# A graph network kernel: one-hots of source and destination made and stored during the dense product, marks summed as rows

## The chip, the cores and the metric

The kernel runs on one core of a Trainium2 chip. The metric is the device time of one execution in microseconds (us). The core has five engines that run side by side: TensorE (PE; its weight loads are PEld), VectorE (DVE), ScalarE (ACT), GpSimd (POOL) and SyncE (SP), which only issues DMAs. An engine works through its own instructions in order; between engines only semaphores order anything.

## The reference

A network of four layers on one graph of 3125 nodes (256 features) and 50000 edges, sorted by destination. Cut to what matters here:

```python
x = _layernorm(x + _L0(x, src, dst, edge_weight, ...))
x = _layernorm(x + _L1(x, ..., edge_attr_3, edge_index))
x = _layernorm(x + _L2(x, edge_index, ...))
x = _layernorm(x + _L3(x, src, dst, ...))

def _L0(x, edge_row, edge_col, edge_weight, weight, bias):
    gathered = edge_weight[:, None] * x[edge_col]
    neigh = segment_sum(gathered, edge_row, num_segments=3125)
    return x @ weight[:256] + neigh @ weight[256:] + bias

def _L1(...):   # attention with 8 heads, the alpha of an edge:
    alpha = sum(h[src] * a_src) + sum(h[dst] * a_dst) + sum(relu(edge_attr @ edge_W.T + edge_b) * h[dst])
    alpha = where(alpha >= 0, alpha, 0.2 * alpha)
    ...         # softmax over the edges of a destination, then the weighted sum of h[src]
```

`_L2` is one plain graph convolution and two attention layers with 4 heads, `_L3` three layers of plain neighbour sums with dense layers between them.

## The kernel before, in words

Layer 0 is computed as a dense product: the 3125 x 3125 matrix of edge weights is built in HBM (`t_w`) and multiplied with x. A second matrix, of edge counts (`t_adj`), serves the plain sums of `_L2` and `_L3`. Both are filled by scatters: an edge that stands for its pair of nodes writes the sum over all edges of this pair. So the stages are, in this order:

**Marks (L1860 to L1895, L888 to L899, L1309 to L1313).** The 50000 edges lie in 98 quads of 4 x 128. For a quad, `compare` on VectorE (and, from quad FIRST = 28 on, on ScalarE for the fourth block) holds the keys of all 512 edges (`wide_key`, loaded by SP from `t_key`, two quads in 512 KB) against the key of each edge: `same_key`, 4 x [128 x 512] in bf16. TensorE multiplies it with `values` (a one and three bf16 parts of the weight): 16 matmuls [128 x 128] by [128 x 4]. `summed` on VectorE reduces them to `w_sum` and `counts` and signals `w_summed`, once a quad.

**Weight scatter (L703).** POOL zeroes nothing itself; `t_w` is zeroed by 13 DMAs of ScalarE. POOL issues 391 indirect DMAs of 128 sums each. Their order (`w_order`) goes by groups of 8 quads: first the first block of each of the 8 quads, then the second, and so on; each waits for `w_summed` of its quad. At most 8 are under way.

**Own product (L906) and pair product (L884).** x times the first half of the weights, then, for 26 tiles of 128 rows of `t_w` (1.6 MB each, loaded by SP at L518 into a ring of four buffers, from the fifth on after `w_out` of two pairs before), 13 pairs of tiles x 13 blocks = 169 blocks. A block is two fp32 matmuls, each two records in the trace; VectorE adds it into `neigh` (L2217). `fold(0)` (L1933, L1934) on VectorE stands between the two and signals `folded0`.

**Zeroing of t_adj (L1333) and adjacency (L720).** ScalarE issues 35 DMAs of 640 KB, ten at once after its last `compare`, the others each after some blocks of the pair product. When all 35 have landed (`adj_zero`) and the counts are there, POOL scatters the counts: 391 indirect DMAs. After them come its gathers.

**First look-up (`look_up`, `encoded`, `edge_scores`).** For every four steps (of 128 edges; 104 times four) SP loads the source and destination numbers, spread over all partitions (`t_hi`, `t_drel`, 128 KB each), ScalarE turns them into one-hots by Abs and Relu (L1362, L1365, and L1366 for an fp32 copy of the destination half), SP stores the bf16 ones as `t_hot` for the later look-ups, and TensorE multiplies node values with them. `t_lo` holds the upper parts of the source numbers, spread by 27 copies from HBM to HBM (L494), which SP issues ahead of its first load of `t_w`.

SP's order around the change: key loads, `t_drel`, `t_hi`, `t_lo1`, the 27 copies, the 26 tiles of `t_w`, then the look-up's loads.

## Time and profile before

| | |
|---|---|
| three runs, median (lowest to highest) | 5571.05 us (5562.35 to 5572.14) |
| the profiled execution's own time | 5553.82 us |
| its span, first to last instruction | 5552.0 us |
| mean granted TensorE clock | 0.792 of full speed |
| busy: PE, PEld, DVE, ACT, POOL | 57%, 35%, 41%, 27%, 37% |
| DMA | 531 MB, 96 GB/s over the span |

Busy is the share of the span in which the engine had an instruction under way. The end of a matmul is modelled in these records, so the time at which a matmul's result was really there is read from the instruction that waited for it. "idle before" and the releaser after an arrow say how long an engine stood still before an instruction and what ended that; "issue" means nothing that the profile shows, and "remote" a source that it doesn't know, which in loops can be another engine of the same core. SPq and ACTq are issues of DMAs.

### The profile page before, as it was taken

To read this page: it belongs to the slowest core of one execution; us is meant where nothing else is said; L and a number is where in the kernel's file an instruction comes from. 1 tells how busy PE (TensorE), PEld (TensorE's weight loads), DVE (VectorE), ACT (ScalarE), POOL (GpSimd) and SP (SyncE) were. 2 spreads that over 40 slices of the span, in tenths; PEclk is the share of its full clock that TensorE was granted. 3 is DMA by queue.
4 is the path that set the end of the run, shared out by engine and by line. 5 is a ranking of instruction groups with operands and counts; after the bars stand their busy time and mean duration, and the time that the engine had idled before them with its cause. 6 is when DMAs were issued, how large, how long until landed. Compare 5 with 4: busy or idle time off the path is not lost. (4 is left out here: it accounts for less than half of the span.)

```text
span 5552.0 us, 64271 instructions
## 1 busy us (share of the span) xinstructions
PE 3182.6 (57%) x16684; PEld 1923.3 (35%) x16685; DVE 2287.2 (41%) x5611; ACT 1485.8 (27%) x3107; POOL 2063.3 (37%) x2093
## 2 busy tenths in 40 slices
PE   2111495332569955457603645771465565999998
PEld 2111342110447733234602522340343333444444
DVE  6222241001359974456202744770475568020213
ACT  0122100000359943235100133550023346030212
POOL 4666406777120056652273056207315540000000
PEclk9999897555779976677756866885676776999999
DMA  9211461000345532232513400014633331313131
GB/s 382 99 40 40 158 253 65 24 21 0 103 124 149 149 88 85 84 90 78 189 33 84 124 21 22 10 37 122 191 103 97 105 118 61 105 61 105 60 109 38
DMA packets 321424, 531.29 MB, mean 96 GB/s; under 512 B 140575, under 2 KB 204664, under 8 KB 317556
## 3 DMA queue, kind: packets, MB, share of 16 engines
q1 hardware_dynamic: 206233, 309.28, 18.0%
q0 software_dynamic: 80624, 130.79, 8.5%
q10 hardware_dynamic: 34381, 89.16, 4.2%
q8 instruction: 66, 1.08, 0.1%
q14 instruction: 120, 0.98, 0.1%
HBM read 410.68 MB, written 121.87 MB: 96 GB/s over the span
## 5 line engine op out<-in xcount | busy, mean ns | idle before, releaser
L1377 ACT ACTIVATE onehot<-iota,drel 128x128 f32<-128x128 f32 x1248 | 381.7, 388 | 1674.4 <-PE ps L1025 762.5
L1102 PE MATMUL ps<-shared_sb,onehot 128*128 128x264 f32 (+1 forms) x1600 | 594.3, 489 | 351.6 <-issue 202.2
L2147 DVE TENSOR_TENSOR accum<-accum,ps 128x264 f32 (+1 forms) x1248 | 527.8, 423 | 493.7 <-issue 315.3
L1162 PE MATMUL ps<-score_sb,shared_sb 128*128 128x512 f16 (+1 forms) x3150 | 628.2, 360 | 20.5 <-DVE shared_sb L2179 20.1
L749 POOL DMA_INDIRECT score_sb<-table,src_x x192 | 200.3, 1043 | 904.0 <-issue 456.5
L1102 PEld LDWEIGHTS ps<-shared_sb,onehot 128*128 128x128 f32 x1600 | 314.0, 228 | 632.4 <-issue 563.5
L720 POOL DMA_INDIRECT t_adj<-counts,early_sb x391 | 400.6, 1025 | 322.8 <-DMA t_adj<-onehot 203.3
L703 POOL DMA_INDIRECT t_w<-early_sb x391 | 390.5, 999 | 232.1 <-DVE counts L1872 131.4
L749 POOL DMA_INDIRECT shared_sb<-table,src_x x360 | 340.3, 945 | 229.2 <-PE ps L1102 119.3
L1162 PEld LDWEIGHTS ps<-score_sb,shared_sb 128*128 128x128 bf16 x3150 | 298.0, 99 | 342.9 <-DVE shared_sb L2179 14.6
L730 POOL TENSOR_SCALAR onehot<-iota,carry_d 98x512 bf16<-98x512 f32 x28 | 43.6, 1561 | 967.3 <-PE ps L1179 804.2
L2217 DVE TENSOR_TENSOR accum<-accum,ps 128x512 f32<-128x512 f32 (+1 forms) x156 | 103.9, 667 | 600.9 <-remote 425.6
L793 POOL DMA_INDIRECT resid_sb<-table,src_x x224 | 212.5, 949 | 361.2 <-DVE shared_sb L2133 243.7
L1002 PE MATMUL ps<-not_lo,lo_hot 128*128 128x400 bf16 x416 | 136.4, 369 | 345.6 <-DVE score_sb L1977 179.0
L1977 DVE TENSOR_REDUCE score_sb<-ps 128x400 f32 x208 | 119.5, 574 | 383.7 <-remote 310.8
L2133 DVE TENSOR_TENSOR shared_sb<-shared_sb,ps 128x256 f32<-128x256 f32 x512 | 211.5, 413 | 83.3 <-issue 55.3
L1023 PE MATMUL ps<-score_sb,onehot 128*128 x832 | 223.1, 412 | 36.5 <-issue 30.0
L897 PE MATMUL ps<-accum,shared_sb 128*128 x784 | 47.6, 171 | 337.7 <-DVE counts L1872 237.6
L749 POOL DMA_INDIRECT resid_sb<-table,src_x x168 | 158.9, 946 | 205.9 <-DMA t_resid<-resid_sb 114.9
L2402 DVE TENSOR_TENSOR accum<-accum,ps 128x1024 f32<-128x1024 f32 (+1 forms) x21 | 23.2, 1107 | 484.2 <-PE ps L1179 484.0
L884 PE MATMUL ps<-resid_sb,score_sb 128*128 128x512 f32 (+1 forms) x336 | 157.6, 614 | 107.5 <-issue 67.1
L1476 ACT ACT_TABLE_LOAD x1 | 1.3, 1283 | 803.5 <-DVE small L1912 803.5
(416 smaller groups left out, 5978.5 us busy)
## 6 DMA issues: line engine op xcount, KB each, us to landing
score_sb<-t_adj SPq DMA_DIRECT2D x105, 640.0 KB, 3.8
accum<-t_hot SPq DMA_DIRECT2D x208, 256.0 KB
t_w<-onehot ACTq DMA_DIRECT2D x13, 3200.0 KB
t_hot<-shared_sb SPq DMA_DIRECT2D x104, 256.0 KB
t_adj<-onehot ACTq DMA_DIRECT2D x35, 640.0 KB
shared_sb<-t_adj SPq DMA_DIRECT2D x35, 640.0 KB, 9.6
resid_sb<-t_w SPq DMA_DIRECT2D x12, 1600.0 KB
accum<-t_hi SPq DMA_DIRECT2D x104, 128.0 KB
```

What stands on the lines that cost most here:

```text
L703: pool.indirect_dma_start(t_w, bass.IndirectOffsetOnAxis(ap=w_x[:, j:j + 1], axis=0), w_sum[:, j:j + 1], None).then_inc((moved + gath)[n % ...
L720: pool.indirect_dma_start(t_adj, bass.IndirectOffsetOnAxis(ap=adj_x[:, j:j + 1], axis=0), counts[:, j:j + 1], None).then_inc((moved + gath ...
L749: pool.indirect_dma_start(to[:, u, 0:w], None, tab, bass.IndirectOffsetOnAxis(ap=src_x[:, step:step + 1], axis=0)).then_inc(landing[0], 16)
L793: pool.indirect_dma_start(x_rows[n % (RG[1] // HU)][:, u, :], None, table[1], bass.IndirectOffsetOnAxis(ap=src_x[:, n * HU + u:n * HU + u ...
L884: mm = pe.matmul(ps[:, m % 8, at:at + now.stop - now.start], lhs, w_ring[t % 4][0:EQ if t == NT else P, now], start=(t == 2 * i), stop=(t ...
L1002: pe.matmul(ps[:, b if k == 0 else q % 2, 0:n_to * NT * H], lo_hot[:, q, :], not_lo[:, to, :].unsqueeze(2).to_broadcast([P, n_to, H, NT]), ...
L1023: mm = pe.matmul(ps[:, 4 + j, 0:GW], hot, hrows[:, bass.ds(at[q * QU + j], 1), :], start=True, stop=True)
L1102: pe.matmul(ps[:, RING[(HU * h + u) % len(RING)], 0:w], onehot[:, h % 2 * HU + u, :], around[g][place(g, i, h)][:, u, 0:w], start=True, st ...
L1162: mm = pe.matmul(ps[:, 2 * (i % 3) + f, 0:w], h_gin[:, t, m, f * P:(f + 1) * P], ring["gin"][:, at % HOLD, c, 0:w], start=(t == 0 and m == ...
L1377: last = act.activation(onehot[:, h % 2 * HU + u, :], iota[:, 0:P], ACT.Abs, bias=drel[:, bass.ds(step + u, 1)], scale=-1.0)
L2133: dve.tensor_tensor(v, of_src, now_w[:, u, 0:H].unsqueeze(2).to_broadcast([P, H, D // H]), ALU.mult).then_inc(msg_ready, 1)
L2147: dve.tensor_tensor(to, to, bank.unsqueeze(1), ALU.add).then_inc(step_acc, 1)
```

## The change

1. **Marks summed as rows.** `values` are spread into `spread_v`, so that the four matmuls of a quad ([128 x 32] weights, `same_key` [128 x 512] moving) add the sums of up to 8 quads as rows of one PSUM bank. A batch (2, 2, 4, eleven times 8, and 2 quads) is copied (`rows_summed`), turned by four transposes (`sums_turned`) and reduced (`summed`), and `w_summed` is signalled once a batch. The loops over quads are unrolled; FIRST is 44, so ScalarE joins the comparisons later.
2. **One-hots earlier.** ScalarE makes the 104 pairs of one-hots after its comparisons and `folded0` (`one_hots`). SP loads their rows (`step_rows`) and stores the results (`keep`), four of each ahead of each tile of `t_w`. The zeroings of `t_adj` go out from the same loop, one behind every second step.
3. **The 27 copies to t_lo** are issued ahead of tile 4 of `t_w`, no longer ahead of tile 0.
4. **First look-up.** SP loads `t_hot` (256 KB) in place of `t_hi` and `t_drel`, stores nothing, and ScalarE only copies the destination half to fp32.

The diff, cut to its core:

```diff
-FIRST = 28
-LOOPED = QUADS // 2 - FIRST // 2
+FIRST = 44
+LOOPED = 35
+BATCHES = [2, 2, 4] + [8] * 11 + [2]
+START = [sum(BATCHES[:n]) for n in range(len(BATCHES) + 1)]
+WIDE = 8 * 36
...
+            sp.wait_ge(*count("key_out", 48))
+
+            def step_rows(n):
+
+                if n >= 2:
+                    sp.wait_ge(*count("apart", n - 1))
+                for j, of in enumerate((t_hi, t_drel)):
+                    sp.dma_start(rows_in[n % 2][:, j, :], on_each(of, n * QU, QU)).then_inc(w_in[4 + n % 2], 16)
+
+            def keep(n):
+
+                sp.wait_ge(*count("hot_k", n + 1))
+                sp.dma_start(t_hot[n:n + 1, :, :].rearrange("a p e -> p (a e)"), hot_k[:, n % 2, :, :].rearrange("p n e -> p (n e)")).then_inc(hot_kept[n % 2], 16)
+
+            by_steps = t_lo.rearrange("n (j r) e -> (n j) r e", j=QU)
+            step_rows(0)
             for t in range(WT):
                 rows_t = EQ if t == NT else P
+                for n in range(4 * t, 4 * t + 4):
+                    if n + 1 < S // QU:
+                        step_rows(n + 1)
+                    keep(n)
+                if t == 4:
+                    for i in range(S // UN + 1):
+                        sp.dma_start(by_steps[i * UN:(i + 1) * UN], t_lo1[i * UN:(i + 1) * UN, :].unsqueeze(1).to_broadcast([UN, P // QU, P])
+                                     ).then_inc(done("lo_out"), 16)
...
+                    sp.wait_ge(*count("src_mm", 4 * i + max(q - 1, 0)))
                     sp.sem_inc(done("sp_go"), 1)
-                    for j, t in enumerate((t_hi, t_drel)):
-                        sp.dma_start(wide[:, q, j, :], on_each(t, i * UN + q * QU, QU)).then_inc(wide_in[q], 16)
+                    sp.dma_start(wide[:, q, :, :].rearrange("p n e -> p (n e)"), t_hot[bass.ds(4 * i + q, 1), :, :].rearrange("a p e -> p (a e)")).then_inc(wide_in[q], 16)
...
-                    pool.wait_ge(*count("w_summed", j // L0H + 3))
+                    pool.wait_ge(*count("w_summed", j // L0H + 1))
...
+            def marks(n, k):
+
+                kk = k - START[n]
+                pe.wait_ge(*count("same_dve", k + 1))
+                pe.wait_ge(*count("same_act", k + 1))
+                if kk == 0:
+                    pe.wait_ge(*count("spread_v", n + 1))
+                    if n >= 2:
+                        pe.wait_ge(*count("sum_rows", n - 1))
+                for b in range(L0H):
+                    mm = pe.matmul(ps[0:32, 4 + n % 2, :], spread_v[n % 2][:, b * WIDE + kk * 32:b * WIDE + kk * 32 + 32], same_key[k % 2][:, b, :],
+                                   start=(kk == 0 and b == 0), stop=(kk == BATCHES[n] - 1 and b == L0H - 1))
+                mm.then_inc(done("quad_sum"), 1)
+
+            def sums_turned(n):
+
+                pe.wait_ge(*count("sum_rows", n + 1))
+                if n >= 2:
+                    pe.wait_ge(*count("w_summed", START[n - 1]))
+                for u in range(L0H):
+                    mm = pe.transpose(ps[:, 6 + n % 2, u * 32:u * 32 + 32], sum_rows[n % 2][:, u * P:(u + 1) * P], ident[0:32, 0:32])
+                mm.then_inc(done("sums_tp"), 1)
+
+            for n in range(len(BATCHES)):
+                for k in range(START[n], START[n + 1]):
+                    marks(n, k)
+                    if n > 0 and k == START[n]:
+                        sums_turned(n - 1)
+            sums_turned(len(BATCHES) - 1)
...
-            for k in range(LOOPED):
-                if k >= 10:
-                    act.wait_ge(*count("w_out", BLOCKS * ((k - 10) // 3) + 1))
-                act.dma_start(cells[k:k + 1, :, :].rearrange("k p w -> p (k w)"), nothing).then_inc(done("adj_zero"), 16)
+            for k in range(FIRST, QUADS):
+                compare(k)
+            def one_hots(n):
+
+                act.wait_ge(w_in[4 + n % 2], 32 * (n // 2 + 1))
+                if n > 0:
+                    act.wait_ge(*count("hot_k", n))
+                act.activation(apart[:, :, :], rows_in[n % 2], ACT.Abs, bias=iota_m[:, :]).then_inc(done("apart"), 1)
+                act.wait_ge(*count("apart", n + 1))
+                if n >= 2:
+                    act.wait_ge(hot_kept[n % 2], 16 * (n // 2))
+                act.activation(hot_k[:, n % 2, :, :], apart[:, :, :], ACT.Relu, bias=ones[:, 0:1], scale=-1.0).then_inc(done("hot_k"), 1)
+
+            act.wait_ge(*count("folded0", 1))
+            act.wait_ge(*count("quad_sum", QUADS))
+            for n in range(S // QU):
+                one_hots(n)
+                if n % 2 == 0 and n // 2 < LOOPED:
+                    k = n // 2
+                    act.dma_start(cells[k:k + 1, :, :].rearrange("k p w -> p (k w)"), nothing).then_inc(done("adj_zero"), 16)
...
-                        act.wait_ge(wide_in[q], 32 * (i + 1))
+                        act.wait_ge(wide_in[q], 16 * (i + 1))
                         act.wait_ge(*count("dst_mm", n + 1))
-                        act.wait_ge(*count("hot_s", n + UN // QU))
-                        act.wait_ge(*count("hot_k", n + 1))
-                        act.activation(apart[:, :, :], wide[:, q, :, :], ACT.Abs, bias=iota_m[:, :]).then_inc(done("apart"), 1)
-                        act.wait_ge(*count("apart", n + 1))
-                        act.wait_ge(hot_kept[q % 2], 8 * (4 * i + q - q % 2) + 16)
-                        act.activation(hot_k[:, q % 2, :, :], apart[:, :, :], ACT.Relu, bias=ones[:, 0:1], scale=-1.0).then_inc(done("hot_k"), 1)
-                        act.activation(hot_t[:, q % 2, :], apart[:, 1, :], ACT.Relu, bias=ones[:, 0:1], scale=-1.0).then_inc(done("hot_s"), 1)
+                        act.activation(hot_t[:, q % 2, :], wide[:, q, 1, :], ACT.Copy).then_inc(done("hot_s"), 1)
...
+            def values_spread(n):
+
+                if n >= 2:
+                    dve.wait_ge(*count("quad_sum", START[n - 1]))
+                to = spread_v[n % 2].rearrange("p (b k x) -> p b k x", b=L0H, x=36)[:, :, 0:BATCHES[n], 0:4]
+                of = values[:, L0H * START[n]:L0H * START[n + 1], :].rearrange("p (k b) v -> p b k v", b=L0H)
+                dve.tensor_copy(to, of).then_inc(done("spread_v"), 1)
+
+            def rows_summed(n):
+
+                dve.wait_ge(*count("quad_sum", START[n + 1]))
+                if n >= 2:
+                    dve.wait_ge(*count("sums_tp", n - 1))
+                dve.tensor_copy(sum_rows[n % 2], ps[0:32, 4 + n % 2, :]).then_inc(done("sum_rows"), 1)
+
+            def summed(n):
+
+                now = slice(START[n], START[n + 1])
+                dve.wait_ge(*count("sums_tp", n + 1))
+                by_quad = ps[:, 6 + n % 2, 0:L0H * 32].rearrange("p (u k v) -> p k u v", u=L0H, v=4)[:, 0:BATCHES[n]]
+                dve.tensor_reduce(w_sum[:, L0H * now.start:L0H * now.stop].rearrange("p (k u) -> p k u", u=L0H), by_quad[:, :, :, 1:4], AX.X, ALU.add)
+                dve.tensor_copy(counts_by[:, now, :], by_quad[:, :, :, 0]).then_inc(done("w_summed"), BATCHES[n])
...
+            for n in range(len(BATCHES)):
+                values_spread(n)
+                for k in range(START[n], START[n + 1]):
+                    compare(k)
+                    if n > 0 and k < START[n] + 2:
+                        (rows_summed, summed)[k - START[n]](n - 1)
```

## Rows read from the trace of the kernel before

**Rows 1.** Busy us by stretch: PE, PEld, DVE, ACT, POOL (count), PEclk, DMA share, GB/s.

```profile
55.00:613.00 558.00, 92.55 (x1538) 70.81 (x1539) 172.57 (x537) 117.16 (x157) 360.43 (x360) 1.00 0.31 108
...
673.00:856.00 183.00, 183.00 (x475) 85.05 (x474) 74.66 (x112) 0.00 (x0) 0.00 (x0) 1.00 0.62 234
856.00:892.00 36.00, 31.87 (x85) 14.59 (x83) 7.98 (x12) 0.00 (x0) 27.18 (x29) 1.00 0.25 92
892.00:1377.00 485.00, 145.43 (x165) 47.05 (x165) 34.20 (x42) 0.00 (x0) 373.44 (x363) 0.53 0.05 13
...
1600.00:1900.00 300.00, 289.97 (x1966) 229.46 (x1965) 272.64 (x342) 282.34 (x303) 0.00 (x0) 1.00 0.57 149
```

**Rows 2.** Groups by line, POOL, 856 to 1400: busy, mean ns, idle before, releasers.

```profile
L720 POOL DMA_INDIRECT t_adj<-counts,early_sb x391 | 400.6, 1025 | 322.8 <-DMA t_adj<-onehot 203.3 <-issue 119.5
```

**Rows 3.** Order of time, 596 to 660 us: start, length, what, idle before, releaser.

```profile
610.67 41.38 SPq L494 DMA_DIRECT2D t_lo<-t_lo  x27
...
652.03 0.96 POOL L703 DMA_INDIRECT t_w<-early_sb  x1 [1.32 <-issue]
```

**Rows 4.** Order of time, end of the t_adj scatters.

```profile
1375.32 1.10 POOL L720 DMA_INDIRECT t_adj<-counts,early_sb  x1 [0.30 <-issue]
...
1403.78 1.02 DVE L2217 TENSOR_TENSOR accum<-accum,ps 128x512 f32<-128x512 f32 x2 [1.43 <-remote]
```

**Rows 5.** Groups by line, 0 to 700 us.

```profile
L703 POOL DMA_INDIRECT t_w<-early_sb x391 | 390.5, 999 | 232.1 <-DVE counts L1872 131.4 <-issue 98.9 <-DMA t_w<-early_sb 1.2
...
L1871 DVE TENSOR_REDUCE early_sb<-ps 128x12 f32 (+1 forms) x98 | 16.2, 165 | 366.5 <-remote 323.1 <-PE ps L897 35.6 <-issue 7.6
```

**Rows 6.** Order of time, marks, 369 to 409 us.

```profile
374.86 1.04 PE L897 MATMUL ps<-accum,shared_sb 128*128 x16 [3.04 <-issue]
...
402.33 0.95 POOL L703 DMA_INDIRECT t_w<-early_sb  x1 [0.30 <-issue]
```

**Rows 7.** Order of time, marks, 400 to 426 us.

```profile
407.18 0.17 DVE L1871 TENSOR_REDUCE early_sb<-ps 128x12 f32 x1 [24.92 <-remote]
...
407.75 0.96 POOL L703 DMA_INDIRECT t_w<-early_sb  x1 [4.47 <-DVE counts L1872]
...
411.00 0.24 SPq L476 DMA_DIRECT2D shared_sb<-t_key  x1
...
414.68 1.28 ACT L1309 ACT_TABLE_LOAD   x1 [1.42 <-DMA shared_sb<-t_key]
```

**Rows 8.** Order of time, pair product beside the t_adj scatters.

```profile
1004.05 0.69 DVE L2217 TENSOR_TENSOR accum<-accum,ps 128x512 f32<-128x512 f32 x1 [10.51 <-remote]
...
1015.25 0.69 DVE L2217 TENSOR_TENSOR accum<-accum,ps 128x512 f32<-128x512 f32 x1 [10.51 <-remote]
```

**Rows 9.** Order of time, pair product without scatters.

```profile
752.81 0.69 DVE L2217 TENSOR_TENSOR accum<-accum,ps 128x512 f32<-128x512 f32 x1 [1.03 <-PE ps L884]
...
754.53 0.69 DVE L2217 TENSOR_TENSOR accum<-accum,ps 128x512 f32<-128x512 f32 x1 [1.03 <-PE ps L884]
```

**Rows 10.** Order of time, a later look-up beside gathers.

```profile
2877.59 0.57 DVE L1977 TENSOR_REDUCE score_sb<-ps 128x400 f32 x1 [35.89 <-remote]
```

**Rows 11.** Groups by line in the first look-up, 1600 to 1900 us.

```profile
L1365 ACT ACTIVATE shared_sb<-score_sb,ones 128x1024 bf16<-128x1024 f32 x76 | 87.3, 1148 | 11.7 <-DMA t_hot<-shared_sb 7.1
L1362 ACT ACTIVATE score_sb<-accum,iota_m 128x1024 f32<-128x1024 bf16 x75 | 85.3, 1137 | 0.0
...
L1369 ACT ACTIVATE accum<-ps 128x1024 f32<-128x1024 f32 x76 | 76.6, 1007 | 6.1 <-PE ps L994 6.0
...
L1366 ACT ACTIVATE onehot<-score_sb,ones 128x512 f32<-128x512 f32 x76 | 53.7, 706 | 0.0
```

**Rows 12.** Busy time in one stretch, beside two loads of t_w.

```profile
693.00:704.00 11.00, 11.00 (x27) 4.83 (x26) 4.21 (x7) 0.00 (x0) 0.00 (x0) 1.00 0.90 327
```

**Rows 13.** VectorE in order of time, end of fold(0).

```profile
672.88 0.69 DVE L1934 TENSOR_REDUCE score_sb<-score_sb 128x16 f32<-128x512 f32 x1
```

More of the change, by code:

```diff
@@ L491, in _ @@
             sp.wait_ge(*count("rows_out", 48))
-            by_steps = t_lo.rearrange("n (j r) e -> (n j) r e", j=QU)
-            for i in range(S // UN + 1):
-                sp.dma_start(by_steps[i * UN:(i + 1) * UN], t_lo1[i * UN:(i + 1) * UN, :].unsqueeze(1).to_broadcast([UN, P // QU, P])
-                             ).then_inc(done("lo_out"), 16)
             sp.wait_ge(*count("need", 1))
@@ L677, in _ @@
             pool.memset(zeros, 0.0).then_inc(done("zeroed"), 1)
+            pool.memset(resid_sb[:, 0:4 * WIDE], 0.0).then_inc(done("zeroed"), 1)
             pool.wait_ge(*count("te", 1))
@@ L734, in looked_up @@
                 def looked_up():
-                    for h in range(2):
-                        pool.wait_ge(hot_kept[h], 16 * (S // QU // 2) + 16)
                     pool.wait_ge(*count("sc_dv", 2 + S // QU))
@@ L888, in _ @@
             pe.wait_ge(*count("adj_ev", 1))
-            with pe.Fori(0, QUADS // 2) as i:
-                for h in range(2):
-                    k = 2 * i + h
-                    pe.wait_ge(*count("same_dve", k + 3))
-                    pe.wait_ge(*count("same_act", k + 1))
-                    pe.wait_ge(*count("w_summed", k + 1))
-                    for u in range(L0H):
-                        for b in range(L0H):
-                            mm = pe.matmul(sums_out[h][:, u, :], same_key[h][:, b, u * P:(u + 1) * P],
-                                           values[:, bass.ds(L0H * k + b, 1), :].rearrange("p j v -> p (j v)"), start=(b == 0), stop=(b == L0H - 1))
-                    mm.then_inc(done("quad_sum"), 1)
+            def marks(n, k):
[23 more added lines that the diff above has]
+            sums_turned(len(BATCHES) - 1)
             def own_product(t):
@@ L1290, in _ @@
             act.sem_inc(done("enc_done"), 2)
-            act.sem_inc(done("hot_k"), 1)
-            act.sem_inc(done("key_used"), FIRST + 2)
+            act.sem_inc(done("key_used"), FIRST)
             act.sem_inc(done("same_act"), FIRST)
-            for h in range(2):
-                act.sem_inc(hot_kept[h], 16)
             act.wait_ge(*count("zeroed", 1))
@@ L1858, in attr_rest @@
                 link(dve.tensor_tensor(attr_g, attr_g, attr_b[:, :, m, :], ALU.subtract))
-            def compare(i, q, tiles=L0H - 1):
-                k, h = 4 * i + q, q % 2
-                dve.wait_ge(key_in[q // 2], 16 * i + 16)
-                dve.wait_ge(*count("quad_sum", k + 1))
-                for u in range(tiles):
-                    last = dve.tensor_scalar(same_key[h][:, u, :], wide_key[q // 2][:, h, :], adj_f[:, bass.ds(k * L0H + u, 1)], None, ALU.is_equal)
-                last.then_inc(done("same_dve"), 1)
@@ L1868, in summed, with compare @@
-            def summed(k, h):
-                dve.wait_ge(*count("quad_sum", k + 3))
-                dve.tensor_reduce(w_sum[:, bass.ds(L0H * k, L0H)], sums_out[h][:, :, 1:4], AX.X, ALU.add)
-                dve.tensor_copy(counts_by[:, bass.ds(k, 1), :], sums_out[h][:, :, 0].unsqueeze(1)).then_inc(done("w_summed"), 1)
+            def compare(k):
+                h = k % 2
+                dve.wait_ge(key_in[k // 2 % 2], 16 * (k // 4) + 16)
+                if k >= 2:
+                    dve.wait_ge(*count("quad_sum", k - 1))
+                for u in range(L0H if k < FIRST else L0H - 1):
+                    last = dve.tensor_scalar(same_key[h][:, u, :], wide_key[k // 2 % 2][:, h, :], adj_f[:, k * L0H + u:k * L0H + u + 1], None, ALU.is_equal)
+                last.then_inc(done("same_dve"), 1)
@@ L1886, in _ @@
-            with dve.Fori(FIRST // 4, QUADS // 4) as i:
-                for q in range(4):
-                    compare(i, q)
-                    summed(4 * i + q - 1, 1 - q % 2)
-            for q in range(QUADS % 4):
-                compare(QUADS // 4, q)
-                summed(QUADS // 4 * 4 + q - 1, 1 - q % 2)
-            summed(QUADS - 1, 1)
-            dve.wait_ge(*count("w_summed", QUADS + 2))
+            dve.wait_ge(*count("zeroed", 2))
+            for n in range(len(BATCHES)):
[4 more added lines that the diff above has]
+                        (rows_summed, summed)[k - START[n]](n - 1)
+                    if k == 7:
+                        dve.wait_ge(*count("attr_rows", 16 * SB))
+                    if k < len(early_work):
+                        early_work[k]()
+                    if k == len(early_work):
+                        dve.tensor_copy(attr_b[:, :, 2, :], attr_g).then_inc(done("attr_split"), 1)
```

92 lines of the change are left out of this document (37 added, 55 removed).

## The prediction

> **What bounds the kernel now.** I read the busy time by stretch first. The opening 1400 us hold three things one after the other [rows 1]: marks and weight sums (55 to 613 us, POOL 65% busy, TensorE 17%), the pair product (673 to 856 us, TensorE busy throughout), and the t_adj scatters (from 856 us, POOL 77% busy, TensorE with 165 matmuls in 485 us). The groups of POOL then say what lets the last of them begin: 203.3 us of idle time were ended by a DMA into t_adj, the zeroing [rows 2]. POOL's last weight scatter starts at 652.0 us [rows 3], so the adjacency starts at 652.0 + 1.0 + 203.3 = 856.3 us. It ends at 1375.3 + 1.1 = 1376.4 us, and the last block of the pair product is added at 1404 to 1405 us [rows 4]; everything later in the kernel comes after that. The end of this stage is therefore the start of the t_adj scatters, plus 520 us, plus what TensorE has left. The groups of the first 700 us show the marks: POOL spends 390.5 us in 391 scatters and 98.9 us between them, 1.25 us each, 489 us in all, and waits 131.4 us for counts L1872 (24 of them before its first scatter, so 107 us later) [rows 5].
>
> **A hold on TensorE, seen in three places.** While POOL issues scatters or gathers back to back, matmuls finish late. In the marks the quad that TensorE starts at 374.86 us isn't read by VectorE until 407.18 us, after POOL has run dry with the scatter at 402.33 us [rows 6, 7]. In the pair product VectorE adds a block of four matmuls every 15.25 - 4.05 = 11.2 us beside scatters [rows 8], but every 1.72 us without them [rows 9]: 2.8 us a matmul. A later look-up, in bf16 and of other shapes, waits 35.9 us for its 13 matmuls, 2.8 us each again [rows 10]. So I take 2.8 us per matmul instruction, whatever its size. It sets in late: VectorE still adds 12 blocks in the first 36 us of scatters [rows 1], 48 matmuls where 36 / 2.8 = 13 would be held ones, so some 35 pass before the hold is full. A POOL pause of about 4 us clears it (402.33 + 0.95 to 407.18) [rows 6, 7].
>
> **Marks (16 matmuls a quad become 4).** Eight quads give 32 scatters, 40 us. Before, they need 128 matmuls; after, 32 and four transposes, 36. A 40 us run of POOL lets through 35 + 14 = 49 from a clear state but only 14 when the hold is full. Two groups need 72 and get 63, so POOL still pauses about every second group: 4 us to clear, some 4 us for the last quads, some 3 us for the copy, the transposes and the reduction. That is 11 us in two groups, about 65 us in 12, in place of 107. Against it stands that the sums now come in batches: group 0 needs batches 2, 2 and 4 and two further compares before its eighth scatter, at about 3.5 us a quad while t_w is being zeroed 15 to 25 us. Net -20 us. Bounds: no pauses after that start, -85; a pause of 12 us in each group, +60. VectorE's added copies (0.7 us each) and the lost reductions lie beside POOL's scatters and cost nothing; if POOL never waits they are covered entirely. What was in the loops is unrolled; instruction loading isn't seen as a wait now and I take it at nothing, up to +10.
>
> **One-hots during the pair product.** This is the part that decides. The 35 zeroing DMAs are now issued by ScalarE after one_hots(0), (2), ... (68), where ten went out at once and the rest followed the blocks. ScalarE's 104 pairs cost 1.14 + 1.15 us each, 238 us on an engine with no work in these stretches [rows 1, 11]; but their chain is longer. SP issues the rows of step n+2 only behind keep(n), which waits for hot_k of n. A load of 512 KB issued at 411.00 us lets its reader start at 414.68 us [rows 7], 3.7 us; the two loads here are half of that together but 1 KB a piece, and I take 3.7 us too. With 0.4 us for the store's issue, 0.4 for the first load's and 2.3 us of ScalarE, two steps take 6.8 us, one step 3.4 us, the four steps that go before each tile of t_w 13.6 us. Behind them the tile's load stands on the same queue ahead of the next rows: 9.9 us of full DMA (0.90 of 11 us) moved 3.6 MB in the stretch with two loads [rows 12], so 1.6 MB takes 4.5 us. The two zeroings of 0.64 MB add 3.6 us of traffic, of which I take 1. Per tile 13.6 + 4.5 + 1 = 19 us, where the pair product alone needs 6.5 x 1.72 = 11.2 us. Bounds: all latency hidden, only traffic counts: look-up traffic of 0.57 x 300 / 76 = 2.25 us a step (with the attributes) [rows 1] makes 4 x 1.9 + 4.5 + 3.6 = 15.7 us; nothing hidden, 13.6 + 4.5 + 3.6 = 21.7 us. Step 68 comes after 17 tiles: 17 x 19 + 3 = 326 us.
>
> The t_lo copies move too: SP needs 41.4 us to issue the 27 of them, before it gets to any tile [rows 3]. Now they stand at tile 4, inside this chain, and keep(20) and all behind it wait; +41 us (bounds 20 to 45). The chain begins at folded0, which needs the own product; it was signalled at 672.88 + 0.69 = 673.6 us [rows 13]. So the scatters begin 326 + 41 = 367 us after folded0 instead of 856.3 - 673.6 = 183 us: +184 us (bounds +110 and +235). That folded0 itself comes 20 us earlier is counted above.
>
> **What TensorE has left.** At the start of the scatters tiles 0 to 16 are there, so 8 pairs or 104 of 169 blocks are done. Before, it was 28 us from POOL's last scatter to the last block [rows 4]. I take +15, bounds 0 and +35.
>
> **First look-up.** ScalarE works 1.15 + 1.14 + 1.01 + 0.71 = 4.0 us per four steps in 300 / 76 = 3.95 us and is the bound there [rows 11]; 2.3 us of it go. TensorE is at 290 of 300 us and VectorE at 273 [rows 1], so the pitch can fall only to some 3.75 us: 0.2 x about 85 groups, -15 us (bounds -25 and 0). The load of ready one-hots replaces two loads and a store.
>
> **The sum.** -20 + 184 + 15 - 15 = +164 us. On the profiled execution of 5553.8 us that is 5718 us; the median of the three runs lies 17 us higher, 5571.05, and I forecast in its terms: 5735 us. With the bounds of the terms not all at one end, its own range is 5630 to 5830.
>
> The Trainium skill (DMA: Bandwidth & Descriptors, Anatomy of one DMA) gives a DMA a fixed cost of about 2.0 us plus its bytes at 436 GB/s. By it a pair of row loads would land after about 2.6 us, an estimate from that page; the trace shows 3.7 us for 512 KB where the page gives 3.2, and by the page's figure the sum would be some 35 us lower.
>
> **Rival 1: the chain runs at the pace of the traffic.** Tiles take 15.7 us, t_lo overlaps (20 us), POOL hardly pauses in the marks: 17 x 15.7 + 3 + 20 = 290, +107 - 85 - 15 = about 5578 us. For it speaks that two row buffers allow overlap; against it that keep(n) stands ahead of the rows of n+2 on SP. Chance 0.12, of which 0.03 faster, 0.04 the same, 0.05 slower.
>
> **Rival 2, on the other side: TensorE runs ahead of POOL.** If four long matmuls escape the hold, quads follow the key loads (4 in 7.7 us); the marks are done near 280 us, own product and one-hots follow while POOL still scatters, and the zeroing is finished before POOL is, at about 580 us. The scatters start 276 us earlier; TensorE has some 136 blocks left, 56 pass beside them, 80 x 1.72 = 138 us remain: 5571 + (580 + 520 + 138 - 1404) - 15 = about 5390 us. It decides once TensorE gets more than 36 matmuls through in 40 us of scatters for good. Against it: three kinds of matmul are held alike [rows 6, 8, 10]. Chance 0.10. The Trainium skill (SBUF — State Buffer, section SBUF: two separate sides) says that on the engine side only the port pair shared by VectorE and GpSimd is contended and TensorE never waits there; by that rule this rival would win. The trace does not show such freedom.
>
> **Rival 3: the batches hurt.** POOL pauses 12 us in each group as TensorE stays behind: marks +60 instead of -20, 5571 + 244 = 5815 us. For it: a group now waits for all its eight quads. Chance 0.08. That the change does nothing of what it says is excluded by the diff.
>
> **How the numbers follow.** Forecast 0.70, rivals 0.12, 0.10 and 0.08. Of this kernel a measurement can tell about 0.2%, 11 us, from no change. Faster 0.03 + 0.10 = 0.13, same 0.04, slower 0.70 + 0.05 + 0.08 = 0.83. The range 5565 to 5830 leaves out rival 2, the low edge of rival 1 and the high edges of the rest.
>
> **What would show it.** Right: t_adj scatters from about 1000 to 1040 us with POOL idle some 380 us before them on the zeroing; TensorE idle between tiles in the pair product; tiles 17 to 21 us apart; weight scatters ending near 635 us with a pause every second group; a look-up pitch near 3.75 us. Wrong: zeroing finished before 900 us, or marks that end long before POOL's scatters.

## The result, and the profile after

The changed kernel takes 5702.95 us (median of four runs, 5677.19 to 5780.38) against 5569.11 us of the kernel before (four runs, 5562.35 to 5572.14): a ratio of 1.023, with a 95% interval of 1.0209 to 1.0251. It is slower by some 130 us, inside the range of 5565 to 5830 and 32 us below the forecast of 5735. Ratios leave out an execution that lies over 1.5% above the fastest of its kernel: the 5780.38 us here and 5759.03 us in e4 below. The profiled execution is that slowest one, 5780.38 us with a span of 5778.5, and lies 77 us above the median. The traced execution of e1, the same kernel again, took 5786.78 us, one of two above 5780 there, so no trace shows what an execution near 5700 us looks like.

Busy time by stretch of the changed kernel (columns as in [rows 1]):

```profile
64.00:635.00 571.00, 195.92 (x536) 67.64 (x534) 172.30 (x421) 74.24 (x109) 402.23 (x391) 0.62 0.29 99
645.00:1043.00 398.00, 189.79 (x448) 86.96 (x448) 69.28 (x105) 158.38 (x138) 0.00 (x0) 0.74 0.74 227
1043.00:1563.00 520.00, 173.86 (x221) 59.16 (x221) 29.56 (x45) 80.32 (x70) 398.59 (x391) 0.54 0.23 63
1563.00:1610.00 47.00, 29.42 (x60) 12.58 (x61) 19.75 (x23) 0.00 (x0) 0.11 (x1) 0.68 0.00 0
1800.00:2100.00 300.00, 282.56 (x1914) 223.31 (x1913) 264.19 (x330) 114.08 (x148) 0.00 (x0) 1.00 0.31 81
```

The pair product before the scatters took 183 us with TensorE busy throughout [rows 1]; now the stretch is 398 us long and TensorE is busy in 190 of them. POOL's groups on the page say why the scatters come so late, and the order of time gives the first and the last scatter and the last block, the end of the stage:

```profile
L734 POOL DMA_INDIRECT t_adj<-counts,early_sb x391 | 398.6, 1019 | 528.9 <-DMA t_adj<-onehot 408.0
L717 POOL DMA_INDIRECT t_w<-early_sb x391 | 402.5, 1029 | 201.4 <-issue 127.6
```

```profile
1043.15 0.95 POOL L734 DMA_INDIRECT t_adj<-counts,early_sb  x1 [407.98 <-DMA t_adj<-onehot]
...
1561.56 1.09 POOL L734 DMA_INDIRECT t_adj<-counts,early_sb  x1 [0.30 <-issue]
...
1609.23 0.42 DVE L2268 TENSOR_TENSOR accum<-accum,ps 128x256 f32<-128x256 f32 x1 [0.20 <-PE ps L898]
```

POOL waits 408 us for the zeroing where it waited 203 [rows 2]. folded0 comes at 645.1 us instead of 673.6. So the stage's end moves by: folded0 -28.5, from folded0 to the first scatter 398.1 instead of 182.7 (+215.4), the scatters 519.5 instead of 520.1 (-0.6), what TensorE has left 47.0 instead of 28.4 (+18.6). That is +204.9 us, 1609.65 against 1404.8 [rows 4]. The first look-up adds 8.5 us, everything behind it 13. Together that is the 226.5 us between the two spans (5778.5 and 5552.0); between the medians lie 134 us.

The chain ahead of the tiles, SP and ScalarE in order of time (L539 loads a tile, L509 rows, L514 stores one-hots):

```profile
659.28 0.33 SPq L539 DMA_DIRECT2D score_sb<-t_w  x1
659.65 0.43 SPq L509 DMA_DIRECT2D score_sb<-t_hi  x1
...
669.09 1.15 ACT L1362 ACTIVATE score_sb<-score_sb,iota_m 128x1024 f32<-128x1024 bf16 x1 [5.25 <-DMA score_sb<-t_drel]
...
671.44 0.34 SPq L514 DMA_DIRECT2D t_hot<-shared_sb  x1
...
671.82 0.43 SPq L509 DMA_DIRECT2D score_sb<-t_hi  x1
...
677.05 1.15 ACT L1362 ACTIVATE score_sb<-score_sb,iota_m 128x1024 f32<-128x1024 bf16 x1 [3.21 <-DMA score_sb<-t_drel]
...
680.50 0.32 SPq L539 DMA_DIRECT2D shared_sb<-t_w  x1
...
748.33 19.39 SPq L526 DMA_DIRECT2D t_lo<-t_lo  x27
```

Tiles are 21.2 us apart here and 22.0 on average from tile 4 (768.45 us) to tile 16 (1032.4 us). Rows that are issued right behind a tile are read 669.09 - 659.65 = 9.4 us later, the others 5.2 us later. The copies to t_lo take SP 19.4 us, not 41.4 [rows 3].

### The profile page after: what moved, and what is told of

Read it like the earlier page. It is cut to its first block and busy times, and to the rows that moved or that the text cites. A ratio compares the mean times of both kernels' runs of the same rounds, so it can differ in the third digit from the quotient of the medians.

```text
span 5778.5 us, 59942 instructions
## 1 busy us (share of the span) xinstructions
PE 3285.9 (57%) x15568; PEld 1902.6 (33%) x15569; DVE 2286.2 (40%) x5491; ACT 1453.0 (25%) x3059; POOL 2073.5 (36%) x2094
## 5 line engine op out<-in xcount | busy, mean ns | idle before, releaser
L717 POOL DMA_INDIRECT t_w<-early_sb x391 | 402.5, 1029 | 201.4 <-issue 127.6
L898 PE MATMUL ps<-resid_sb,score_sb 128*128 128x512 f32 (+1 forms) x336 | 194.5, 711 | 300.8 <-issue 237.4
L1044 PE MATMUL ps<-accum 128*128 128x100 bf16 (+1 forms) x3744 | 308.1, 238 | 38.3 <-issue 38.1
L1044 PEld LDWEIGHTS ps<-accum 128*128 128x128 bf16 x3744 | 272.6, 107 | 71.2 <-issue 44.7
L898 PE MATMUL ps<-score_sb 128*128 128x512 f32 (+1 forms) x196 | 114.5, 659 | 250.6 <-issue 171.1
```

The lines of the kernel that those rows point to most:

```text
L717: pool.indirect_dma_start(t_w, bass.IndirectOffsetOnAxis(ap=w_x[:, j:j + 1], axis=0), w_sum[:, j:j + 1], None).then_inc((moved + gath)[n % ...
L898: mm = pe.matmul(ps[:, m % 8, at:at + now.stop - now.start], lhs, w_ring[t % 4][0:EQ if t == NT else P, now], start=(t == 2 * i), stop=(t ...
L1044: mm = pe.matmul(out, hot, src_b8[:, m, :] if k == 0 else src_b[:, m, :, :], start=False, stop=(m == 2 and (j % 2 == 1 if k == 0 else j == ...
```

## The experiments

A ratio compares a kernel with the kernel before run beside it on the same chip (before: 5596 us for e1 to e4, 5597 for e5 to e8, 5603 for e9 to e11, 5557 for e12), so times are to be compared by their ratios. "Stage end" is the last block of the pair product in the profiled execution. A block is one of the 169 units of the pair product, four pairs of a weight load and a matmul, added up by VectorE once; "the hold" is the state in which TensorE gets through them about six times more slowly (11.2 us a block, not 1.72).

| | median, us | ratio, 95% interval | stage end, us |
|---|---|---|---|
| e1 changed kernel again | 5754 | 1.0265 (1.0220 to 1.0309) | 1592 |
| e2 marks only | 5577 | 0.9949 (0.9927 to 0.9971) | 1357 |
| e3 one-hots only | 5821 | 1.0409 (1.0394 to 1.0424) | 1634 |
| e4 changed, zeroings at once | 5723 | 1.0248 (1.0223 to 1.0273) | 1448 |
| e5 marks, zeroings at once | 5557 | 0.9941 (0.9912 to 0.9969) | 1345 |
| e6 e4, one-hots on ScalarE's queue | 5577 | 0.9947 (0.9922 to 0.9973) | 1384 |
| e7 e5, POOL waits every 32nd | 5405 | 0.9671 (0.9635 to 0.9707) | 1209 |
| e8 before, zeroings at once | 5605 | 1.0013 (1.0004 to 1.0023) | 1424 |
| e9 e6 paced as e7 | 5423 | 0.9666 (0.9636 to 0.9697) | 1244 |
| e10 e5, POOL waits every 16th | 5416 | 0.9667 (0.9636 to 0.9698) | 1196 |
| e11 e5, POOL waits every 4th | 5212 | 0.9306 (0.9261 to 0.9352) | 936 |
| e12 e8, POOL waits every 4th | 5212 | 0.9389 (0.9369 to 0.9408) | 982 |

**Which part loses (e1 to e3).** e1 is the changed kernel without an edit. e2 is the kernel before with part 1 alone, e3 with parts 2 to 4 alone.

> The changed kernel again, unaltered, for a profile of an ordinary run of it. Every theory expects 5680 to 5715 us. If the long chain of one-hots sets the start of the t_adj scatters, they start about 365 to 400 us after folded0, tiles of t_w are loaded 19 to 22 us apart, and nearly all of the added time lies ahead of the end of the pair product (1404 us before).

> The kernel before with part 1 of the change alone: marks summed as rows, FIRST 44, loops over quads unrolled; one-hots, zeroing, t_lo and first look-up stay as before. My theory, that this part is worth -20 to -28 us and the loss is all in the other parts, expects 5540 to 5555 us. The rival that the batches hurt POOL expects up to 5630 us. If TensorE were free of the hold with long matmuls (the rival on the fast side), own product and zeroing would be done near the end of the weight scatters: below 5500 us.

> The kernel before with parts 2 to 4 of the change alone; the marks are made as before. If the parts add up, it takes the changed kernel's time plus what the marks gain: 5700 to 5730 us, with t_adj scatters about 1060 us. If the marks part of the change is itself a loss, it is faster than the changed kernel: below 5680 us.

e1 shows folded0 at 629 us, scatters from 1024.4 us, 395 us later, tiles 22 us apart, stage end 1592: the same picture. Its four runs go from 5722 to 5790 us; the median of 5754 misses the expected 5680 to 5715, of which the chip explains 27 us (the kernel before takes 5596 there, 5569 in the first comparison). The marks gain 0.5%, 28 us by the ratio and 19 by the medians, about as expected; the one-hots alone cost 4.1%, 229 us, more than the 130 to 160 us that I had expected. -0.5 and +4.1 make +3.6, where both together cost 2.3 to 2.7, so the parts don't quite add up: in e3 the scatters start 40 us later than in e1 (1064.9), since its marks and folded0 come later by 47 us (676 and 629 us). The marks alone were worth more there than the 28 us of e2.

**Is it the zeroing that hangs on the one-hots? (e4, e5)** e4 is the changed kernel, e5 is e2, each with the zeroings moved. The edit in e4:

```diff
+            for k in range(LOOPED):
+                act.dma_start(cells[k:k + 1, :, :].rearrange("k p w -> p (k w)"), nothing).then_inc(done("adj_zero"), 16)
             act.wait_ge(*count("folded0", 1))
             act.wait_ge(*count("quad_sum", QUADS))
             for n in range(S // QU):
                 one_hots(n)
-                if n % 2 == 0 and n // 2 < LOOPED:
-                    k = n // 2
-                    act.dma_start(cells[k:k + 1, :, :].rearrange("k p w -> p (k w)"), nothing).then_inc(done("adj_zero"), 16)
```

> The changed kernel with one thing moved: ScalarE issues all 35 zeroings of t_adj right behind its last comparison, ahead of its wait for folded0 and of the one-hots. Theory (the chain of one-hots delays the scatters only because the zeroings hang on it): POOL goes from the weight scatters straight on to the t_adj scatters near 640 us, they end near 1160 us, some 60 blocks pass beside them, 109 x 1.72 = 187 us remain, the stage ends near 1350 us instead of 1610, and the kernel takes about 5515 us (5490 to 5560). Rival (the chain ahead of each tile sets the end whatever the zeroing does, or the scatters only push the same work elsewhere): within 20 us of the changed kernel, about 5690 us.

> The marks-only kernel (e2) with all 35 zeroings of t_adj issued at once behind ScalarE's last comparison; no one-hots ahead of the look-up. e4 ended the stage at 1448 us where 1350 were expected, and its tiles came 20 us apart behind the last t_adj scatter. If it was the one-hots ahead of each tile that kept e4 back, this kernel reaches what e4 missed: t_adj scatters from about 640 to 1160 us, some 67 blocks beside them, 102 x 1.72 = 175 us left, stage end near 1335 us, 20 us before e2: 5555 us against e2's 5577. Rival (while POOL scatters, TensorE loses more than it gains by the earlier start): stage end at 1357 us or later, 5577 us or more.

My expectation of e4 failed. The 400 us wait is gone, scatters run from 642.6 to 1171.7 us, yet the kernel takes 5723 us and not 5515, against 5754 for e1. e5 came out as expected, 5557 us. Busy time beside and behind the scatters (columns as in [rows 1]), e4 first, then e5:

```profile
643.00:1171.00 528.00, 168.28 (x192) 54.81 (x192) 29.91 (x45) 73.47 (x64) 406.72 (x391) 0.55 0.22 57
1171.00:1450.00 279.00, 172.11 (x405) 79.13 (x405) 73.46 (x102) 98.78 (x86) 0.82 (x2) 0.79 0.50 151
```

```profile
640.00:1169.00 529.00, 168.66 (x192) 54.75 (x192) 29.84 (x45) 0.00 (x0) 405.52 (x391) 0.54 0.09 25
1169.00:1345.00 176.00, 156.84 (x398) 72.45 (x396) 71.62 (x100) 0.00 (x0) 0.46 (x2) 0.92 0.29 110
```

Beside the scatters both do the same 45 blocks. Behind them e5 needs 176 us (1.76 a block, no wait for tiles), e4 279 us for the same work with TensorE busy in 172: its tiles come 20 us apart, as SP's order shows:

```profile
1199.37 0.32 SPq L539 DMA_DIRECT2D resid_sb<-t_w  x1
1219.29 0.32 SPq L539 DMA_DIRECT2D resid_sb<-t_w  x1
1239.46 0.32 SPq L539 DMA_DIRECT2D score_sb<-t_w  x1
```

While POOL scatters, SP waits ahead of a tile for a free buffer, and the one-hots stand behind that wait; they are made up for afterwards, ahead of each tile. So the one-hots hold the stage up twice over: through the zeroings, and through their place on SP's queue. Removing the first exposes the second. The traced run of e4 is moreover the fastest of its four (5646 to 5759), with comparisons that ended at 271 us; where the others lost more wasn't seen.

**The same one-hots on a queue of their own (e6).** ScalarE issues the rows itself, behind its Abs, and the store behind its Relu; SP only loads tiles, and `step_rows` and `keep` are gone from its loop. Two more things change with it: rows are asked for ahead of the Relu and not behind the store, and the copies to t_lo stand ahead of tile 12 and not of tile 4:

```diff
                 act.activation(apart[:, :, :], rows_in[n % 2], ACT.Abs, bias=iota_m[:, :]).then_inc(done("apart"), 1)
                 act.wait_ge(*count("apart", n + 1))
+                if n + 2 < S // QU:
+                    step_rows(n + 2)
...
+                act.wait_ge(*count("hot_k", n + 1))
+                act.dma_start(t_hot[n:n + 1, :, :].rearrange("a p e -> p (a e)"), hot_k[:, n % 2, :, :].rearrange("p n e -> p (n e)")).then_inc(hot_kept[n % 2], 16)
```

> e4 with the one-hots taken off SP's queue: ScalarE issues the row loads, the stores and nothing waits ahead of a tile; SP only loads tiles, with the t_lo copies ahead of tile 12. If e4's loss lies in the order on SP (a tile waits for four steps, four steps wait for a free tile buffer), the stage ends as in e5, near 1335 to 1350 us, and the kernel takes 5550 to 5570 us. If the one-hots' own traffic and ScalarE's 2.3 us a step are the cost wherever they stand, it ends near e4's 1448 us, 5640 us or more.

```profile
638.00:1166.00 528.00, 165.43 (x191) 54.34 (x191) 29.48 (x44) 220.31 (x192) 401.27 (x392) 0.53 0.49 115
1166.00:1385.00 219.00, 199.13 (x497) 90.70 (x497) 87.39 (x124) 0.00 (x0) 0.55 (x2) 0.93 0.38 134
```

All of the loss is gone: 0.9947, where e2 has 0.9949 and e5 0.9941. The median, 5577 us, lies just above the 5550 to 5570 expected and far from the rival's 5640. ScalarE does nearly all of its one-hots (192 of 208 instructions) beside the scatters, at no cost that can be measured; the stage of the traced run ends 39 us after that of e5, with comparisons that ended at 443 us and not at 325; the medians lie 20 us apart (5577 and 5557), the intervals of the ratios overlap almost wholly. So the price was the place of the one-hots ahead of the tiles on SP's queue, not their work; what the earlier requests and the later t_lo copies have of it wasn't tried apart. But nothing is gained either: with the look-up's one-hots ready, e6 is no faster than e5.

**The hold (e8, e7, e10).** e5 starts the scatters 166 us before e2 and ends the stage 12 us before it. e8 asks the same of the kernel before; its edit is the one wait left out that the zeroings had from the 11th on.

> The kernel before with all 35 zeroings issued at once; nothing else of the change. If the start of the t_adj scatters sets the stage's end by the sum of POOL's 520 us and what TensorE has left, scatters run from about 655 to 1175 us, 102 x 1.72 = 175 us remain, the stage ends near 1350 us instead of 1405: 5545 us on this chip, against 5596. Rival (gated zeroing cost nothing, since TensorE's work is only put off): 5590 to 5600 us.

It gained nothing: 1.0013, 5605 us, as the rival said and not the 5545 us that I expected. The scatters run from 685.2 to 1206.0 us, 170 us earlier than before, and 218 us of pair product remain behind them instead of 28 [rows 4]: only 44 of the 169 blocks pass beside them. In the middle of e5, in order of time, POOL and TensorE go in step:

```profile
899.45 1.09 POOL L722 DMA_INDIRECT t_adj<-counts,early_sb  x1 [0.30 <-issue]
899.87 1.01 PE L885 MATMUL ps<-shared_sb,score_sb 128*128 128x512 f32 x1 [1.79 <-issue]
900.85 1.10 POOL L722 DMA_INDIRECT t_adj<-counts,early_sb  x1 [0.30 <-issue]
901.27 0.28 PEld L885 LDWEIGHTS ps<-score_sb 128*128 128x128 f32 x1 [2.51 <-issue]
902.25 1.10 POOL L722 DMA_INDIRECT t_adj<-counts,early_sb  x1 [0.30 <-issue]
902.68 1.01 PE L885 MATMUL ps<-score_sb 128*128 128x512 f32 x1 [1.80 <-issue]
```

Here one instruction of TensorE, a weight load or a matmul, starts 0.42 us after each scatter, and the 2.8 us per matmul of the prediction are a load and a matmul of 1.40 us each. But it isn't the scatter that lets the instruction go. Three stretches of e5, the hold early and in the middle of the scatters, then behind the last of them (1169.35 us), and VectorE's blocks there:

```profile
701.00:781.00 80.00, 26.73 (x29) 8.15 (x29) 4.80 (x7) 0.00 (x0) 60.72 (x64) 0.50 0.02 0
861.00:941.00 80.00, 27.04 (x29) 8.31 (x29) 4.80 (x7) 0.00 (x0) 62.62 (x58) 0.50 0.02 0
1171.00:1194.00 23.00, 6.36 (x9) 2.49 (x10) 1.38 (x2) 0.00 (x0) 0.00 (x0) 0.50 0.00 0
```

```profile
1177.09 0.69 DVE L2248 TENSOR_TENSOR accum<-accum,ps 128x512 f32<-128x512 f32 x1 [9.11 <-remote]
1188.29 0.69 DVE L2248 TENSOR_TENSOR accum<-accum,ps 128x512 f32<-128x512 f32 x1 [10.51 <-remote]
```

TensorE starts 58 instructions in 80 us both times, one in 1.40 us, while POOL issues 64 DMAs in the first stretch, at 1.26 us, and 58 in the second, at 1.40. POOL comes down to TensorE's pace only after 144 scatters; in the kernel before after 195, 246 us from the first. And the hold outlives the last scatter by 24 us (by 23 to 27 us in every run without a wait between the scatters in which TensorE's records show it). These numbers fit a backlog: something gets through one DMA in 1.40 us while POOL issues one in 1.26, falls behind by 0.14 us each time, 195 x 0.14 = 27 us in all, and then slows POOL down. That is an estimate from these rows; what it is that falls behind, and how it holds TensorE, no record shows.

e7 makes POOL wait for TensorE now and then, e10 twice as often for half as much:

```diff
                     if j >= 2 * NACC:
                         pool.wait_ge(*written(1, j - 2 * NACC))
+                    if j % 32 == 0 and j > 0:
+                        pool.wait_ge(*count("w_out", BLOCKS * (j // 32)))
```

> e5 with one wait more on POOL: ahead of every 32nd t_adj scatter it waits until TensorE is through with one more pair of tiles (13 blocks). My claim that a pause of some 4 us clears the hold and about 35 matmuls (9 to 12 blocks) then pass expects pauses of 4 to 7 us, scatters that take 520 + 12 x 6 = 590 us, 12 or 13 blocks per 32 scatters beside them and almost nothing left: stage end near 1250 us, 85 us before e5, about 5470 us. Rival (a pause clears nothing, TensorE only works while POOL stands still): 4 blocks per 32 scatters pass, 9 x 1.72 = 16 us of pause each, scatters take 710 us, the stage ends near 1365 us, 30 us behind e5.

> e7 with the wait ahead of every 16th scatter, for half a pair each. In e7 the held pace went on for 6 us after POOL's last scatter, then came 18 blocks at 1.72 us, and 24 us after POOL had started again TensorE was held again. If a pause has to last 6 us before it clears anything, 24 short pauses cost more than they free: 20 to 60 us slower than e7. If only the share of time without scatters counts, the same as e7 within 10 us.

e7 in order of time, TensorE and POOL around one pause, then VectorE's blocks:

```profile
816.74 0.95 POOL L724 DMA_INDIRECT t_adj<-counts,early_sb  x1 [0.30 <-issue]
828.14 0.95 POOL L724 DMA_INDIRECT t_adj<-counts,early_sb  x1 [10.45 <-remote]
```

```profile
821.56 1.01 PE L887 MATMUL ps<-shared_sb,score_sb 128*128 128x512 f32 x1 [1.79 <-issue]
823.66 1.01 PE L887 MATMUL ps<-shared_sb,score_sb 128*128 128x512 f32 x1 [1.09 <-issue]
824.47 1.06 PE L887 MATMUL ps<-score_sb 128*128 128x512 f32 x1
```

```profile
826.48 6.05 DVE L2250 TENSOR_TENSOR accum<-accum,ps 128x512 f32<-128x512 f32 x10 [2.82 <-remote]
...
843.68 0.69 DVE L2250 TENSOR_TENSOR accum<-accum,ps 128x512 f32<-128x512 f32 x1 [1.03 <-PE ps L887]
...
860.70 0.69 DVE L2250 TENSOR_TENSOR accum<-accum,ps 128x512 f32<-128x512 f32 x1 [8.75 <-remote]
871.13 0.69 DVE L2250 TENSOR_TENSOR accum<-accum,ps 128x512 f32<-128x512 f32 x1 [9.75 <-remote]
```

The claim that a pause clears the hold stands: 5405 us where 5470 were expected, ratio 0.967, 190 us faster than the kernel before. After POOL's last scatter ahead of the pause (817.7 us) the held pace goes on for 6 us, and 32 x 0.14 = 4.5 us is what the backlog would be; then VectorE gets 17 blocks in 18 us, and about 20 us after POOL has started again TensorE is held anew. Pauses twice as often (e10) bring the same; the expectation that they cost 20 to 60 us fell.

**What sets it in (e11, e12).** If it is a backlog, a slightly slower POOL should never build it up. e11 is e5 with a small wait instead of pauses; e12 has the same wait in e8, so none of the change.

```diff
+                    if j % 4 == 0 and j > 0:
+                        pool.wait_ge(*written(1, j - 1))
```

> e5 with POOL waiting ahead of every 4th t_adj scatter until the one before has landed (2.1 us after its start): a mean pitch of some 1.55 us in place of 1.26 to 1.40, no pause over 2.5 us. In e5 TensorE starts exactly one instruction per scatter, a weight load or a matmul, while POOL's pitch is 1.40 us. If the hold comes from a backlog that fills at a pitch of 1.26 us and needs some slack to drain, it never sets in: all blocks pass beside the scatters (391 x 1.55 = 606 us), stage end near 1250 us, about 5445 us. If only pauses of 4 us and more clear it, TensorE still does one instruction per scatter, scatters end 80 us later than in e5 and the stage ends near 1400 us: 5610 us.

> The kernel before with two edits and nothing of the change: all zeroings at once (e8) and the wait ahead of every 4th t_adj scatter (e11). If e11's gain comes from the pacing alone, this kernel lies behind e11 only by its later start of the t_adj scatters, 685 us in e8 against 642: 5212 + 43 = 5255 us. If the marks summed as rows had a share in the gain beyond that start, 5300 us or more.

e11, POOL in order of time and as a group, then busy time beside the pair product and beside the first look-up:

```profile
657.04 0.95 POOL L724 DMA_INDIRECT t_adj<-counts,early_sb  x1 [0.30 <-issue]
658.30 0.96 POOL L724 DMA_INDIRECT t_adj<-counts,early_sb  x1 [0.31 <-issue]
661.18 0.96 POOL L724 DMA_INDIRECT t_adj<-counts,early_sb  x1 [1.92 <-DMA t_adj<-counts,early_sb]
```

```profile
L724 POOL DMA_INDIRECT t_adj<-counts,early_sb x391 | 381.4, 975 | 422.4 <-DMA t_adj<-counts,early_sb 318.0 <-issue 104.4
```

```profile
641.00:683.00 42.00, 17.00 (x17) 4.60 (x16) 2.08 (x3) 0.00 (x0) 24.50 (x26) 0.50 0.01 0
683.00:937.00 254.00, 250.76 (x648) 116.61 (x649) 110.88 (x159) 0.00 (x0) 121.62 (x122) 0.99 0.38 141
937.00:1443.00 506.00, 402.47 (x2480) 309.77 (x2479) 338.91 (x485) 356.39 (x427) 234.93 (x245) 0.96 0.49 115
```

For the first 42 us TensorE is still held, with 33 instructions (the weight scatters ahead of it, back to back until 640 us, have no wait). From 683 us on it isn't: busy in 250.8 of 254 us, at full clock (0.99 granted where it was 0.54), while POOL scatters 122 times beside it. The pair product is done at 936 us; the scatters take 800 us instead of 527 (2.05 us each: every 4th starts 2.9 us after the one before while nothing else is loaded, and 5 to 8 us after it at many places beside tiles) and run on into the first look-up, which starts without them. 5212 us, 6.9% faster than the kernel before, and 230 us better than expected, since I had the rest of the kernel wait for the scatters. The wait makes POOL slower on average and at the same time lets the scatters under way land every 4th time; which of the two does it isn't told apart. e12 takes 5212 us against 5557 on its own chip, 0.9389, without any part of the change; on e11's chip that would be 0.9389 x 5603 = 5261 us against 5255 expected. Both beat both kernels, and the distance between them, 0.8% and measured on two chips, is about what the marks as rows are worth.

**All parts, paced (e9).** e6 with e7's edit.

> e6 (all parts of the change, one-hots on ScalarE's own queue, zeroings at once) with the pacing of e7: POOL waits ahead of every 32nd t_adj scatter for one more pair of tiles. If the one-hots are harmless once they stand on a queue of their own, stage end near e7's 1209 us and a time within 15 us of e7's 5405. If their 104 x 2.3 us of ScalarE and their traffic hurt, or the first look-up really gains 15 us, it shows here: 5430 us or more, or 5390 or less.

0.9666 against e7's 0.9671: the one-hots are harmless there and worth nothing, though the traced run ends the stage at 1244 us and not near 1209.

## Why the prediction was right, and where it was not

**The total** is closer than its terms. The forecast sum was +164 us in terms of a traced execution. In the traced one the terms are -28.5 (forecast -20), +215.4 (+184), -0.6, +18.6 (+15), +8.5 (-15) and +13 behind the look-up (nothing), +226.5 in all, 62 us too many. The median comes to +134 because the other three executions took 66 to 103 us less, and where they save it wasn't traced. That the median landed 32 us from the forecast is in part luck. What the experiments bear out is the direction and the term that decides.

**The chain** was right in kind: the scatters wait for the zeroing and the zeroing for the one-hots, +215 us where +184 was forecast (bounds 110 and 235). Two terms were off against each other. A tile took 22 us, not 19: the second pair of steps took 9.05 us (671.82 to 680.87) instead of 6.8, as two loads of rows are read after 5.2 us and not 3.7; the pair behind a tile took 12.2 us as forecast. 17 x 3 = 51 us. Without zeroings (e4) tiles come 20 us apart, so these cost some 2 us a tile where 1 was taken. t_lo took 19.4 us where 41 was carried over from a stretch whose issue was slower; -20 us. The Trainium skill (DMA: Bandwidth & Descriptors, Anatomy of one DMA) would have had the rows after an estimated 2.6 us. That section fits its figure to DMAs that GpSimd issues, while these loads are SP's; they were read after 5.2 us.

But the reading that the start of the scatters, plus 520 us, plus a rest decides the stage was too narrow. e4 took the delay away and got back 0.2 of 2.7%, less than the intervals can tell, because the same work delays the tiles; e6 got it all.

**The marks** gained as forecast, -20 against -28 at folded0, -18 at the last weight scatter (634.22 against 652.03 us [rows 3]) and 28 us in e2. How they gain was not as forecast. A quad is held as before, four long matmuls taking 11.2 us:

```profile
328.67 1.89 PE L913 MATMUL ps<-accum,resid_sb 128*32 128x512 bf16 x4 [9.34 <-ACT accum L1342]
...
339.83 1.89 PE L913 MATMUL ps<-shared_sb,resid_sb 128*32 128x512 bf16 x4 [9.27 <-issue]
```

So 2.8 us whatever the size is confirmed by a fourth kind of matmul, and rival 2 fell: once the hold is there, long matmuls do not escape it. Yet POOL pauses for over 4 us only twice past 100 us, at 348.5 and 438.8 us, not in every second group, and the comparisons end at 489 us, long before the scatters, which I had named a sign that I was wrong. From 60 to 200 us POOL's pitch is 1.7 us (81 instructions in 140 us), there is no hold, and TensorE has some 48 quads done by 205 us, more than twice what POOL has scattered. The own product behind the marks is then held in turn until POOL is done, so folded0 comes only 10 us after the last scatter. And POOL is slower, 1.35 us a scatter instead of 1.25 [rows 5], 41 us in all, which eats half of the 80 us of waits for counts that were saved.

**The count of 35 matmuls** that pass first was wrong; the hold comes with time. In e8 the tiles come late and only 3 blocks pass before the hold is there at 721 us, 36 us after the scatters' start as in [rows 1]; in e7 it is back some 20 us after a pause, with 17 blocks passed. That a pause of 4 us clears the hold is true of short runs of scatters alone: 6 us behind 32 of them, some 25 us behind 391.

**What is left** behind the scatters was +18.6 us for a forecast of 15, but the forecast counted it as free work. Some 25 of the 47 us are still held, as were 25 of the 28 us before, when VectorE added only five blocks; the right size is luck. **The first look-up** did not gain 15 us. Its pitch went from 3.95 to 4.05 us (74 groups in 300 us, 76 before). I had set TensorE's floor at 3.75 us, but 290 busy us over 76 groups [rows 1, 11] are already 3.8; TensorE was as much the bound as ScalarE, and freeing ScalarE could give 0.1 us at most. In e1 TensorE waits for VectorE and for the fp32 copy of ScalarE about 0.13 us each per group:

```profile
L1055 PE MATMUL ps<-score_sb,onehot 128*128 x588 | 154.1, 405 | 9.5 <-ACT onehot L1401 9.5
...
L1034 PE MATMUL ps<-not_lo,lo_hot 128*128 128x400 bf16 x146 | 38.3, 343 | 9.1 <-DVE score_sb L2044 9.1
```

**Rival 1** gave 15.7 us a tile and is out with 22. **Rival 3**, batches that hurt, is out by e2.

## What to carry to other kernels

Before work is moved into an idle engine, ask whose queue its loads and stores join and what stands behind them: the same one-hots cost 3% ahead of the tile loads (e4) and nothing that shows on a queue of their own (e6). When a delay is taken away, look at once for what comes due next from the same cause. And where one engine runs at a fixed pace beside another that has nothing to do with it, test the pace itself: two lines that make POOL wait were worth more than everything else in this study.

## What the runs showed of the hardware

Beside indirect DMAs that POOL issues back to back, at 1.26 us each, TensorE comes down to one instruction in 1.40 us: 2.8 us for a load and its matmul, the same for the four kinds of matmul seen here. The hold sets in bit by bit, 12 to 36 us after such a run begins. It goes on after the run ends, for 6 us behind 32 DMAs and for 23 to 27 us behind 391. POOL itself is slowed to 1.40 us a DMA after 144 to 206 of them. With a wait for the landing ahead of every 4th DMA (mean pitch 2.05 us) it did not set in again in the pair product; what it had left of the weight scatters was gone after 42 us. The granted clock goes with it: 0.53 to 0.56 over the stretches with scatters, 0.50 where TensorE is held throughout, 0.99 beside paced ones. What the two engines share stays open: no record shows it. The Trainium skill (SBUF — State Buffer, SBUF: two separate sides) says that TensorE's ports never wait for anyone; here TensorE does wait, though these runs can't say that it is for a port.

Kernels with marks as rows vary more from run to run (e5: 5529 to 5604 us) than the kernel before (5583 to 5603 us), and in their traces the comparisons end anywhere between 271 and 508 us (before: 612 us). I take it that the moment at which the hold sets in differs; that isn't shown, as no experiment was made on it.
